# Two-layer graph network on one core: the first 28 gathers read untransformed input rows, are transformed on TensorE later, and the prologue joins the main block

## What is computed

```python
def _L0_gnn_ref(x, edge_index, edge_attr, ...):
    src, dst = (edge_index[0], edge_index[1])
    xl = (x @ W_lin.T).reshape(N, H, C)                 # H = 4 heads, C = 32
    x_j, x_i = xl[src], xl[dst]
    alpha = (x_i * att_src).sum(-1) + (x_j * att_dst).sum(-1) + (ef * att_edge).sum(-1)
    alpha = jax.nn.leaky_relu(alpha, NEG_SLOPE)
    e = jnp.exp(alpha - segment_max(alpha, dst)[dst])
    alpha = e / (segment_sum(e, dst)[dst] + 1e-16)
    out = segment_sum(x_j * alpha[..., None], dst)
    ...
x = _layernorm(x + _L0_gnn_ref(x, ...))
x = _layernorm(x + _L1_gnn_ref(x, ...))
```

## Time and profile before

| | us |
|---|---|
| median of 3 runs | 4197.17 |
| profiled execution, whole | 4202.79 |
| its span | 4199.6 |
| GpSimd busy | 3084.7 (73%) |
| VectorE busy | 2678.5 (64%) |
| TensorE busy (matmul) | 1910.8 (46%) |
| ScalarE busy | 246.5 (6%) |
| first gather of the first layer starts | 35.22 |
| last gather of the first layer starts | 2063.18 |

### The profile page before, as it was taken

How to read it: one execution, slowest core, us unless ns; L and a number is a source line. 1 busy time by engine, 2 the same in 40 slices (tenths; PEclk the granted TensorE clock), 3 DMA queues, 4 the chain that set the end, 5 groups by cost and what they waited for, 6 DMA issues and landing times.

```text
span 4199.6 us, 47127 instructions
## 1 busy us (share of the span) xinstructions
PE 1910.8 (46%) x10492; PEld 1598.2 (38%) x10492; DVE 2678.5 (64%) x5080; ACT 246.5 (6%) x611; POOL 3084.7 (73%) x3263
## 2 busy tenths in 40 slices
PE   3344455544444545444534444444444444444444
PEld 2233333333333333333434444444444444444444
DVE  3355566555555665555657777777777777777776
ACT  1011110101101100011100000000000000000000
POOL 6777777777777777777537777777777777777775
PEclk6666776766667767666765555555555555555555
DMA  7344444444344444444346766666666666766664
GB/s 204 98 120 117 139 139 128 133 127 119 116 128 139 127 139 125 127 120 117 104 158 213 220 217 217 217 218 218 214 215 219 217 218 213 222 213 215 216 219 150
DMA packets 373128, 711.20 MB, mean 169 GB/s; under 512 B 129320, under 2 KB 216664, under 8 KB 372824
## 3 DMA queue, kind: packets, MB, share of 16 engines
q0 software_dynamic: 130160, 326.22, 27.6%
q1 hardware_dynamic: 197896, 354.70, 26.0%
q10 hardware_dynamic: 45024, 29.80, 2.3%
HBM read 682.29 MB, written 28.15 MB: 169 GB/s over the span
## 4 chain that ended last, share of the span: by engine, by line
POOL 36%; issue 21%; DVE 18%; DVEq 10%; PE 9%; DMA 4%; ACT 1%; POOLq 0%; ACTq 0%; SPq 0%
POOL ring L1271 21%; POOL ring L554 14%; DVEq L860 4%; DVE work L863 4%; DMA ring<-kv_table,den_cols 3%; PE psum L1297 3%; PE psum L660 2%; DVE psum L1413 2%; DVE ring L1411 2%; DVE psum L1408 1%; DVEq L71 1%; DVE ring L1422 1%; DVEq L1409 1%; DVE work L960 0%; DVE work L963 0%
## 5 line engine op out<-in xcount | busy, mean ns | idle before, releaser
L554 POOL DMA_INDIRECT ring<-x_table,idx x1612 | 1527.9, 948 | 511.5 <-issue 465.9
L1271 POOL DMA_INDIRECT ring<-kv_table,den_cols x1516 | 1440.2, 950 | 462.1 <-issue 447.1
L1297 PE MATMUL psum<-work,ring 128*128 128x42 f32 x3232 | 735.4, 420 | 1099.1 <-DVE ring L1422 1099.1
L1297 PEld LDWEIGHTS psum<-work,ring 128*128 128x128 f32 x3232 | 704.6, 330 | 1154.7 <-DVE ring L1422 1154.7
L660 PE MATMUL psum<-work 128*42 128x132 f32 x3232 | 488.3, 314 | 194.7 <-DVE work L963 194.6
L660 PEld LDWEIGHTS psum<-work 128*42 128x42 f32 x3232 | 411.1, 136 | 250.6 <-DVE work L963 226.4
L1408 DVE TENSOR_TENSOR psum<-psum,ring 128x1024 f32<-128x1024 f32 x202 | 248.1, 1228 | 340.5 <-DMA ring<-kv_table,den_cols 320.6
L1398 DVE TENSOR_TENSOR work<-dst_all,psum 126x1024 bf16<-126x1024 int32 x202 | 246.6, 1221 | 78.0 <-issue 67.9
L863 DVE TENSOR_TENSOR work<-dst_all,psum 126x1024 bf16<-126x1024 int32 x204 | 249.1, 1221 | 67.3 <-issue 40.8
L1411 DVE TENSOR_TENSOR ring<-psum,ring 128x1024 f32<-128x1024 f32 x202 | 247.4, 1225 | 19.0 <-issue 7.6
L1413 DVE TENSOR_REDUCE psum<-ring 128x64 f32<-128x1024 f32 x202 | 247.9, 1227 | 16.6 <-issue 2.9
(11 more groups left out here) (200 smaller groups left out, 2153.0 us busy)
## 6 DMA issues: line engine op xcount, KB each, us to landing
dst_all<-dst_row_dram SPq DMA_DIRECT2D x406, 512.0 KB, 5.6
ring<-ea_dram SPq DMA_DIRECT2D x202, 512.0 KB, 4.0
ring<-x_table,idx POOLq DMA_INDIRECT x1612
ring<-kv_table,den_cols POOLq DMA_INDIRECT x1516, 2.8
ea_pair<-ea_turned_dram SPq DMA_DIRECT2D x102, 128.0 KB
kv_table<-work ACTq DMA_DIRECT2D x17, 512.0 KB, 3.1
q_table<-work ACTq DMA_DIRECT2D x17, 384.0 KB, 3.9
ring<-q_table SPq DMA_DIRECT2D x202, 31.5 KB
```

The source lines that it names most:

```text
L554: pool.indirect_dma_start(x_rows[:, h * CHUNK_TILES + t, :], None, k["x_table"], bass.IndirectOffsetOnAxis(idx[h][:, t:t + 1], 0))\
L1271: pool.indirect_dma_start(kv[j][:, t, :], None, k["kv_table"], bass.IndirectOffsetOnAxis(index[:, tile:tile + 1], 0))\
L1297: last = pe.matmul(sum_ps[j % 2], message[j % 2][:, t, :], onehot[j][:, t, :], start=t == 0, stop=t == GROUP - 1)
```

## The change

1. The prologue is no longer a block of its own. Its five parts become functions (`prepare_sync` and so on) that each engine runs ahead of its part of the first layer, in one block. Where an engine reads the number of passes it now waits for VectorE's `prologue_over`; GpSimd does so only after its last gather.
2. SP's first load is `idx0` of chunk 0. The 13 loads of constants go from GpSimd's queue to ScalarE's. The memset of the ones and the memset of `denT` go to VectorE.
3. GpSimd gathers the rows of the first 28 tiles of chunk 0 straight from the input `xpad` (128 floats a row) into `raw_rows`: 23 in `work`, 3 in `ahead`, 2 in `back`. Then it waits for all of `x_table` (`rows_out`) and gathers tiles 28 to 95 as before.
4. After the scores of chunk 0, `raw_tiles` transforms these 28 tiles in seven steps of four: TensorE transposes them, ScalarE copies the result to `x_fin`, TensorE multiplies by `rhs0`, ScalarE copies the rows to `x_rows`. `rhs0` now lies in `score`. VectorE waits for the last step (`raw_made`) before `scores_so_far(0)`, which overwrites it.

```diff
+RAW_TILES = 28
+RAW_BATCH = 4
...
-    rhs0 = ring[:, at:at + W0]
-    at += W0
+    rhs0 = score.rearrange("p h t -> p (h t)")[:, 0:W0]
...
-    with nc.Block() as block:
-        @block.sync
-        def _(sp):
...
+    def prepare_sync(sp):
+        sp.dma_start(idx0[0], src_idx0[0, :, :]).then_inc(first_idx_in, 16)
...
+    def prepare_gpsimd(pool):
+        pool.wait_ge(first_idx_in, 16)
+        for t in range(RAW_TILES):
+            pool.indirect_dma_start(raw_rows[t], None, xpad, bass.IndirectOffsetOnAxis(idx0[0][:, t:t + 1], 0))\
+                .then_inc(raw_in, 16)
+        pool.wait_ge(rows_out, 16 * PIECES)
...
+    def prepare_scalar(act):
+        for to, of in ((base_i, base_rep), (last_i, last_rep), (base_sb, base_row), (fin_sb, fin_row), (dst_i, dst_tile)):
+            act.dma_start(to, of).then_inc(ints_in, 16)
...
+        dve.tensor_tensor(out=passes_sb, in0=passes_sb, in1=fin_passes, op=ALU.max).then_inc(prologue_over, 1)
...
-            wait_here(pool, idx_in[h], 16 * (nth + 1), pool_gate)
-            wait_here(pool, rows_released, s + 1, pool_gate)
-            for t in range(tiles):
+            if not first:
+                wait_here(pool, idx_in[h], 16 * (nth if h == 0 else nth + 1), pool_gate)
+                wait_here(pool, rows_released, s + 1, pool_gate)
+            for t in range(RAW_TILES if first else 0, tiles):
...
+        def raw_tiles():
+            pe.wait_ge(k["raw_in"], 16 * RAW_TILES)
+            for i in range(RAW_STEPS):
+                if i:
+                    pe.wait_ge(raw_made, i)
+                for b in range(RAW_BATCH):
+                    last = pe.transpose(raw_ps[:, b * P:(b + 1) * P], k["raw_rows"][i * RAW_BATCH + b], k["ident_sb"])
+                last.then_inc(raw_turned, 1)
+                pe.wait_ge(raw_copied, i + 1)
+                for b in range(RAW_BATCH):
+                    last = pe.matmul(raw_made_ps[b // 2][:, b % 2, :], x_fin[:, b * P:(b + 1) * P], k["rhs0"][:, 0:MROW],
+                                     start=True, stop=True)
+                last.then_inc(raw_rows_set, 1)
...
+        def raw_tiles():
+            for i in range(RAW_STEPS):
+                act.wait_ge(raw_turned, i + 1)
+                act.activation(x_fin, raw_ps, ACT.Copy).then_inc(raw_copied, 1)
+                act.wait_ge(raw_rows_set, i + 1)
+                for half, made in enumerate(raw_made_ps):
+                    rows = x_rows[:, i * RAW_BATCH + 2 * half:i * RAW_BATCH + 2 * half + 2, :]
+                    act.activation(rows[:, :, 0:FEAT], made[:, :, 0:FEAT], ACT.Copy)
+                    last = act.activation(rows[:, :, MROW:XROW], made[:, :, FEAT:MROW], ACT.Copy)
+                last.then_inc(raw_made, 1)
...
             next_pass()
+        dve.memset(k["denT"], 0.0)
+        dve.memset(x_rows[:, 0:RAW_TILES, FEAT:MROW], 1.0)
+        dve.wait_ge(raw_made, RAW_STEPS)
         scores_so_far(0)
```

More of the change, by code:

```diff
@@ L132, in program @@
     work = sb("work", [P, 5 * GROUP * P])
+    score = sb("score", [P, HEADS0, CHUNK_TILES])
+    ahead = sb("ahead", [P, RUN])
+    back = sb("back", [P, RUN])
     dst_all = [sb(f"dst_all{i}", [P, GROUP * P], I32) for i in range(2)]
@@ L320, in program @@
         drel=drel, base_f=base_f, base_sb=base_sb, passes_sb=passes_sb, sumT=sumT, denT=denT,
+        rhs0=rhs0, raw_rows=raw_rows, raw_in=raw_in, prologue_over=prologue_over, ahead=ahead, back=back, score=score,
         we_att=we_att, ring=ring, idx0=idx0, idx0_in=idx0_in, idx1=idx1, work=work, dst_all=dst_all, psum=psum, bank=bank, wide=wide)
```

241 lines of the change are left out of this document (127 added, 114 removed).

## The result

| | kernel before | changed kernel |
|---|---|---|
| median of the runs | 4196.61 us (4193.83 to 4198.04, 4 runs) | 4162.50 us (4160.21 to 4163.62, 4 runs) |
| ratio | 1 | 0.9917, 95% interval 0.9905 to 0.9929 |
| span of the profiled execution | 4199.6 us | 4161.8 us |

34 us faster, with an interval of 30 to 40 us, where the forecast was 28.6. The median of 4162.50 lies only 0.5 us above the lower end of the range of 4162 to 4179. The sign was right, and so was the place of most of the gain, the earlier stream of GpSimd. But a part of it, some 7 us in the profiles, comes from the second layer, which the prediction put at nothing. On two of the chips met later, the same kernel is *slower* than the kernel before (last experiments).

The account below looks back on a forecast made before the run. GpSimd's gather stream was taken to bound the first layer. L890 30.2 us earlier by chain A, less a 1.6 us stop from chain B, gives 28.6 us: 4197.17 - 28.6 = 4168.6 us, range 4162 to 4179.

Parts of the forecast that it names:

- the second layer is untouched: Second layer: the change gains or loses nothing there; a second layer that shifts by itself had chance 0.03.
- chain B: Path through the landing of `ai_table`, chunk 0's scores and the raw steps to L890: releases L890 at 134.2 us.
- d: Delay of the landing of `ai_table` by 28 more gathers on full DMA engines: 7 us, bounds 3 and 12.
- seven raw steps: Serial transposes, matmuls and copies after chunk 0's scores: 5.06 us a step, 35.4 us for seven.
- the stop of 1.6 us: GpSimd held up in chunk 1 by late VectorE: 7.1 us of lateness less 5.5 us of room.
- chain A: GpSimd's stream of chunk 0's gathers up to L890: releases L890 at 127.1 instead of 157.28, 30.2 us earlier.
- GpSimd is the bound of the first layer, and only the start of chunk 0 moves: First layer: gathers at 1.25 us each set the time; VectorE has 17 us to spare per later chunk.
- The term for VectorE's work: Prologue: VectorE instructions beside the raw gathers, mainly L287, lengthen GpSimd's stream by 2 us, bounds 0 and 4.
- The room: Ties of chunk 1's gathers to VectorE, tightest at tile 12: L890 may be 5.5 us late without stopping GpSimd.
- rival (1): Chain A alone decides, by the upper clock or d under 5.4: gain 30 to 33 us, 4164 to 4167; chance 0.22.
- The long memset: Prologue: the 5.39 us memset of `sumT` would not block gathers; if it did, chain A up to 5 us later.
- Rival (4): Slower: prologue stores starve behind gathers, `ai_table` lands later than 77 us; at 90 it gives 4210; chance 0.03.

Follow-up runs that it names:

- last experiments: Changed kernel unaltered, run a third time on a slower chip, against the kernel before there: 4982.58 us against 4953.08, ratio 1.0066.
- the relatives: Variants of the changed kernel (two or seven more raw steps; 0, 8, 20 or 24 raw tiles; loads on GpSimd): ratios 0.9914 to 1.0000.
- the twin: Changed kernel run once more with nothing altered, on the chip of the runs with more raw steps: 4164.31 us, ratio 0.9914 to the kernel before.

## Where the prediction failed, and what of it was right

Two steps of the sum failed. The first is "the second layer is untouched": it stood at nothing without a reason, and measures 6.7 us here and up to 8.3 in the relatives. The second is in chain B: the delay d of `ai_table` stood at 7 us and measures 1 to 4, and seven raw steps are 1.7 us shorter, so the stop of 1.6 us for which the forecast made chain B the bound doesn't come, and chain A alone decides. A smaller miss is in chain A, which is 1.1 us earlier. The forecast of 28.6 and the 37.8 between the two spans are 9.2 us apart: 2.5 in the first layer (31.1) and 6.7 in the second. The medians are 34.1 us apart, since the profiled execution of the kernel before lay 5.6 us above its median and that of the changed kernel 1.0. That the median still lies in the range, by 0.5 us, is luck: the range had no term for the second layer.

- **GpSimd is the bound of the first layer, and only the start of chunk 0 moves.** Right: five kernels with an earlier or later stream (8, 20, 24, 28 raw tiles, loads on GpSimd) follow their stream (from the start of chunk 1 to the end of the layer they all take 1992 to 1997 us), and without raw tiles the first layer gains nothing.
- **Chain A.** First gather forecast at 3.0, measured at 3.21; gather 95 at 122.3 plus 2 for VectorE's work beside it, measured 123.26 in all. The pace of 1.25 us from `xpad` held, and so did gather 28 without a wait. The term for VectorE's work was mis-sized: 2 us forecast, 0.7 us measured (gathers at 25.83, 27.18 and 28.47), though 1.7 in the twin. So chain A gives 126.0 instead of 127.1.
- **Chain B.** This is the step that failed in the first layer. d was forecast at 7 (bounds 3 to 12); it is 4.0 between the two profiles and 3 in the mean of all, at or under its lower bound. A raw step was forecast at 5.06 and is 4.82, 1.7 us over seven. With 4.0 and 4.82 the sum of 134.2 becomes 129.5, and L942 started at 130.0: the rest agreed within 0.5 us. The step's parts were 1.86, 2.09 and 0.91 us by rows of the finish, and measure 1.81, 2.16 and 0.85; the 0.05 for four columns more was there (2.16 against 2.09), the four copies took 0.80 instead of 0.91, and the hop back 0.05 instead of 0.15. d was put midway between the bytes (4.8 us) and the summed time of packets (9.5 us); even the bytes were too dear. The rows fit engines that weren't at their peak after 20 us and could carry more: the kernel before moved 266 GB/s from 20 to 30, the changed one 308 and 309 from 20 to 25 and from 25 to 30.
- **The room.** Forecast 5.5 at tile 12, measured 4.4 there and 4.9 at tile 8 by two runs; the 0.83 us from the end of a scan to the gather behind it was missing. Chain B is late by 4.0, not 7.1, so the stop of 1.6 us doesn't come. The first layer's gain is then 28.6 + 1.6 + 1.1 = 31.3, measured 31.25: rival (1), "chain A alone decides", whose condition "d under 5.4" came true. It had 0.22; with bounds of d from 3 to 12 and a room of 5.5 it deserved about as much as the forecast.
- **"The second layer is untouched."** Wrong by 6.7 us in the profiled executions (2050.1 and 2043.3): its gathers became 4 ns shorter. This had 0.03 in the chances and is larger than any other error. Why they became shorter no run shows.
- **The long memset.** First the rows: the 5.39 us memset of `sumT` at 2.56 held no gather, and the one of `denT` at 90.33 didn't either; L292 (it was L287), with two inputs in SBUF, did. The gather that starts while L292 runs ends 0.82 to 0.83 us after L292's end in all seven profiles in which one does: it takes 1.47 us here (28.47, beside L292 from 27.26 for 1.85), 1.98 us with 24 raw tiles and 2.59 us in the twin. The Trainium skill ("SBUF — State Buffer", section "Who interferes with whom") says that two SBUF inputs contend and a memset doesn't on this chip; by that rule the trace agrees, but for the one gather of 7.03 us beside a memset in the kernel without raw tiles. That one also ends 0.82 us after the end of an instruction with two SBUF inputs, L922, which follows the memset; but L922 alone is too short to have held it from 86.9 to 92.2.
- **Rival (4), stores that starve.** On the first kind of chip it didn't happen. On the second the outcome did, at 29.5 us, by another mechanism than the one given. The Trainium skill ("DMA: Bandwidth & Descriptors", section "Queues, rings and completion order") says that an engine takes turns between its queues; with a DMA share of 0.20 in that stretch it doesn't explain the late table there. The trace agrees with the rule no further than this: no run here shows the turns themselves. Nothing in the trace of before from the first kind of chip could have shown this.

## What to carry to other kernels

When an engine that issues at a fixed pace is the bound, work that it can do ahead of its first input is worth its whole length, but only as far as the second chain that this lengthens fits into the ties behind it; measure that room by making the second chain longer, not by arguing. Raw work ahead needs only as many tiles as cover the wait: 24 gave what 28 did. And a change that keeps one engine busy through a prologue should be tried on more than one chip: here it gained 0.9% on one kind and lost 0.7% on another.

## What the hardware showed that I had not expected

- The same instructions took 4200 us on some chips and 4954 us on two others, where waits of 4 to 9 us in the prologue were put down to "remote" beside raw gathers, and none without raw gathers (ScalarE's L768, beside the gathers of the first layer: 658.5 us "remote").
- The mean duration of a gather of the second layer belongs to the program: 950 ns in both profiles of the kernel before, 945 to 947 in those of the changed kernel and its relatives on the first kind of chip. Over 1612 gathers that is 5 to 8 us, about a fifth of what the change brought there.
- 28 more gathers in a stretch where the DMA share was about 1 (0.98 to 1.06 from 5 to 30 us before) delayed a landing by only 1 to 4 us, less than their bytes take at the 383 GB/s that the kernel before moved from 5 to 10 us (4.8 us).
- A single instruction of VectorE of 1.85 us, with two inputs in SBUF, went with a gather of 2.59 us instead of 0.94, and once a gather took 7.03 us.
- A gather that waits for a scan of VectorE starts 0.83 us after its end, four times out of four.
